# Pair 10 loaded before the last two x pieces, and the small matmuls of a spiking feed-forward kernel one place later

## What is computed

```
rates  = relu(x) * 0.001
c      = cond[:, None, :] + cumsum(rates, axis=1)
spikes = (floor(c) - floor(c one token earlier)) / 0.001
out    = x + relu(spikes @ w1 + b1) @ w2 + b2        # w1 512x2048, w2 2048x512
```

## Time and profile before

| | us |
|---|---|
| median of 3 runs | 106.62 |
| lowest and highest run | 106.08, 106.63 |
| the profiled execution | 106.2 |
| its span | 104.4 |
| TensorE busy | 96.1 (92%) |
| VectorE busy | 66.5 (64%) |
| GpSimd busy | 43.2 (41%) |
| ScalarE busy | 35.4 (34%) |

### The profile page before, as it was taken

The page is one execution under the profiler, slowest core; times in us unless marked ns, Lnnn a source line. Parts: engine busy times, 40 slices in busy tenths (PEclk is TensorE's granted clock), DMA queues, the critical chain, the costliest instruction groups (busy, mean ns, idle before and its releaser), DMA issues.

```text
span 104.4 us, 1157 instructions
## 1 busy us (share of the span) xinstructions
PE 96.1 (92%) x370; PEld 53.5 (51%) x370; DVE 66.5 (64%) x142; ACT 35.4 (34%) x64; POOL 43.2 (41%) x44
## 2 busy tenths in 40 slices
PE   5999999999999994979999999999999999999910
PEld 5844444445544440624244373568999994444300
DVE  2528999988799999288949978899980011200020
ACT  2767525325461505589620000001964440000000
POOL 6340000000088500037329244199977858850030
PEclk9999999999999999999999999999999999999997
DMA  2999999999999999999996987209999999884001
GB/s 73 323 335 402 419 417 409 414 402 414 413 405 401 397 399 404 406 388 387 372 371 255 420 355 298 104 0 420 420 405 402 337 196 226 108 96 61 6 6 61
DMA packets 10028, 31.66 MB, mean 303 GB/s; under 512 B 1671, under 2 KB 1799, under 8 KB 8994
## 3 DMA queue, kind: packets, MB, share of 16 engines
q1 hardware_dynamic: 8304, 29.63, 73.4%
q0 software_dynamic: 1568, 1.90, 11.0%
q10 hardware_dynamic: 146, 0.01, 0.1%
HBM read 21.58 MB, written 10.75 MB: 309 GB/s over the span
## 4 chain that ended last, share of the span: by engine, by line
DMA 25%; SPq 21%; DVE 14%; POOL 14%; issue 12%; PE 8%; ACT 2%; POOLq 0%; DVEq 0%
DMA w_sb<-in_w_pairs 16%; SPq L270 14%; DMA out<-x_sb 9%; POOL x_sb L352 8%; POOL out L345 5%; SPq L265 5%; DVE x_sb L672 4%; PE ps_table L805 4%; DVE same L599 3%; PE ps_idle L821 2%; DVE hot L618 1%; PE ps_idle L831 1%; POOL out L380 1%; PE ps_turn L842 1%; ACT w_sb L422 1%
## 5 line engine op out<-in xcount | busy, mean ns | idle before, releaser
L805 PE MATMUL ps_table<-w_sb 128*128 128x512 f32 x128 | 57.6, 597 | 1.5 <-ACT w_sb L422 1.5
L805 PEld LDWEIGHTS ps_table<-w_sb 128*128 128x128 f32 x128 | 23.4, 190 | 29.0 <-issue 23.9
L340 POOL DMA_INDIRECT rates<-in_x_turned,sixteen_at x8 | 9.9, 1235 | 34.2 <-DVE sixteen_at L562 32.4
L352 POOL TENSOR_TENSOR x_sb<-x_sb,idle_row 128x512 f32<-128x512 f32 x12 | 14.9, 1277 | 10.6 <-DVEq L704 3.7
L421 ACT ACTIVATE w_sb<-w_sb,b_col 128x512 f32<-128x512 f32 (+2 forms) x19 | 12.2, 642 | 17.6 <-DMA w_sb<-in_w_pairs 17.5
L548 DVE SCALAR_TENSOR_TENSOR total_two<-x_sb,total_two 128x1024 f32<-128x1024 f32 x14 | 17.2, 1225 | 0.9 <-DMA x_sb<-in_x 0.5
L893 PE MATMUL ps_table<-w_sb 128*128 128x512 f32 x32 | 14.0, 595 | 0.0
L345 POOL DMA_INDIRECT out<-w_sb,to_single x8 | 12.5, 1557 | 3.4 <-issue 1.8
L422 ACT ACTIVATE w_sb<-w_sb,minus_relu_b 128x512 f32<-128x512 f32 (+2 forms) x19 | 12.3, 649 | 0.6
L672 DVE TENSOR_TENSOR x_sb<-x_sb,ps_idle 128x2048 f32<-128x2048 f32 x5 | 11.2, 2282 | 1.5 <-ACT idle_row L447 1.3
L451 ACT ACTIVATE w_sb<-ps_turn,b_col 128x128 f32<-128x128 f32 x8 | 2.9, 368 | 20.9 <-PE ps_turn L886 20.9
(11 more groups left out here) (113 smaller groups left out, 66.1 us busy)
## 6 DMA issues: line engine op xcount, KB each, us to landing
x_sb<-in_x SPq DMA_DIRECT2D x16, 512.0 KB, 13.9
out<-x_sb SPq DMA_DIRECT2D x8, 1024.0 KB, 4.2
w_sb<-in_w_pairs SPq DMA_DIRECT2D x15, 512.0 KB, 15.5
w_sb<-in_w SPq DMA_DIRECT2D x4, 1024.0 KB, 15.3
w_sb<-in_w_pairs SPq DMA_DIRECT2D x2, 256.0 KB, 2.9
b_row<-in_b SPq DMA_DIRECT2D x1, 256.0 KB, 15.4
rates<-in_x_turned,sixteen_at POOLq DMA_INDIRECT x8
out<-w_sb,to_single POOLq DMA_INDIRECT x8
```

What stands on the lines that cost most here:

```text
L340: pool.indirect_dma_start(out=rates[:, col, :], out_offset=None, in_=x_sixteen, in_offset=bass.IndirectOffsetOnAxis(ap=sixteen_at[:, col:c ...
L352: last = pool.tensor_tensor(x_sb[b][:, t, :], x_sb[b][:, t, :], idle_row[:, :], ALU.add)
L805: last = pe.matmul(ps_table[c][:, :], table_hidden[:, m, c * P:(c + 1) * P], w2_sb[:, m, :], start=(m == 0), stop=(m == FC - 1))
```

## The change

It reorders; nothing is added or taken away.

- SyncE's loads: pair 10 comes after x piece 13, ahead of pieces 14 and 15. The pairs from 11 on come behind piece 15 as before. The stores of batch 0 go 0, 3, 1, 2 instead of 0, 2, 3, 1.
- TensorE: the sums of batch 1 come after three parts of chunk 10 instead of one. The first spread comes after the whole of chunk 11, instead of after chunk 10, and the strips right behind it. The join comes after one part of chunk 12, the first count of leads after three parts of chunk 12. From chunk 13 on, all is as before.
- VectorE: step 8 of the idle row by hand goes between x pieces 13 and 14, ahead of the last two pieces. The quarter of tokens 8 to 11 of batch 0 goes from ahead of the second tokens to behind the second spikes, so that one quarter is added ahead of the second tokens.
- GpSimd adds 2, 2 and 8 single tokens after its three gates, instead of 3, 2 and 7.

```diff
@@ SyncE, loads @@
-            for h in range(13, B * XH):
-                load_x(h)
-            for m in range(10, FC):
+            load_x(13)
+            load_pair(10)
+            load_x(14)
+            load_x(15)
+            for m in range(11, FC):
                 load_pair(m)
@@ SyncE, stores @@
-            for b, q in ((0, 0), (0, 2), (0, 3), (0, 1), (1, 3), (1, 0), (1, 1), (1, 2)):
+            for b, q in ((0, 0), (0, 3), (0, 1), (0, 2), (1, 3), (1, 0), (1, 1), (1, 2)):
@@ GpSimd @@
             pool.wait_ge(reading_psum, 1)
-            add_idle(0, 12, 15)
+            add_idle(0, 12, 14)
             pool.wait_ge(reading_psum, 2)
-            add_idle(0, 15, 16)
-            add_idle(1, 12, 13)
+            add_idle(0, 14, 16)
             pool.wait_ge(reading_psum, 3)
-            add_idle(1, 13, 16)
+            add_idle(1, 12, 16)
             add_idle(1, 8, 12)
@@ VectorE @@
             find_bases(0)
-            block_totals(1, 5, XH)
+            block_totals(1, 5, 6)
             idle_by_hand(8)
+            block_totals(1, 6, XH)
             find_blocks(1)
@@
             add_idle(0, 0, 4)
-            add_idle(0, 8, 12)
             find_tokens(1)
@@
             add_idle(0, 4, 8)
             second_spikes()
+            add_idle(0, 8, 12)
             add_idle(1, 0, 4)
@@ TensorE @@
             table_chunk(9)
-            table_part(10, 0, 1)
+            table_part(10, 0, 3)
             sum_totals(1)
-            table_part(10, 1, DC)
+            table_part(10, 3, DC)
+            table_chunk(11)
             spread_tokens(0)
-            table_part(11, 0, 2)
             add_strips(0, FC - BY_HAND + 1)
-            table_part(11, 2, 3)
+            table_part(12, 0, 1)
             join_strips()
-            table_part(11, 3, DC)
-            table_part(12, 0, 1)
+            table_part(12, 1, 3)
             count_leads(0)
-            table_part(12, 1, DC)
+            table_part(12, 3, DC)
             table_part(13, 0, 3)
             spread_tokens(1)
```

## The result

The changed kernel takes 104.55 us (median of 5 runs, 103.89 to 104.73), the kernel before 106.08 (5 runs, 105.89 to 106.63): a ratio of 0.984, interval 0.9805 to 0.9875. A second set of the same kernel, with before on the same chip, gave 104.31 against 106.30, ratio 0.9846 (0.9801 to 0.9892). By medians it is faster by 1.5 and 2.0 us, by the ratios by 1.6 to 1.7, where 2.9 were forecast. The forecast 103.5 is about 1 us too low, and the measured time lies in the range. Medians in this document are over all executions; ratios leave out executions over 1.5% above the fastest of their kernel, which matters for the small sets (e3).

The account below looks back on a forecast made before the run. TensorE was taken to bound the kernel, with three stalls (1.66, 0.86, 0.36 us) adding to 2.88; the steps gave 2.92 less, span 101.5, time 103.3 or 103.7 by the median, stated as 103.5, range 102.9 to 105.1.

Parts of the forecast that it names:

- Step 1: Loads: pair 10 lands near 37.3, so TensorE's 1.66 us of idleness before chunk 10 goes, with 1.4 in hand.
- Step 2: VectorE's totals: done by 42.3 with 0.5 us cover, second sums on TensorE at 42.84 against 42.80, no gain there.
- Step 3: First spread and strips on TensorE: no wait for tokens, 1.0 us in hand, strips at 48.58, 0.84 earlier.
- Step 4: Join: still bound by strips and ScalarE, 2.87 us after the strips, so at 51.45; idle row's copy ends 53.21.
- Step 5: VectorE's one quarter ahead of second tokens: these come 3.04 us earlier, no TensorE wait, about 0.1 in hand at the count.
- The gather: Gather for the second tokens: lands at 55.3, 5.7 us after issue, against a start of 55.56; cost taken as 0.
- Step 6: From the second count of leads: old order, 5.73 us to the first layer, which starts at 68.27, 2.92 us earlier.
- Step 7: GpSimd and stores: last tile near 74.3, batch 1's scatters end near 93.5, last scatter with 4 us in hand.
- C: Rival: x piece 15 lands late and delays the second sums; 104 to 105.2 us, chance 0.09.
- D: Rival: no change, the stores set the end or the gaps return elsewhere; 106.6 us, chance 0.06.
- E: Rival: slower, piece 15 so late that the whole chain from the totals slips; 106.6 to 108.1 us, chance 0.06.
- B: Rival: second tokens late, by GpSimd's two tiles (first mechanism) or a late gather; 103.7 to 104.8 us, chance 0.17.

Follow-up runs that it names:

- e3: Changed kernel with the quarter of tokens 8 to 11 of batch 0 back ahead of the second tokens; 105.44 us, ratio 0.9885.
- e2: Changed kernel with the order of loads and VectorE's step 8 put back as before; 105.04 us, ratio 0.9888.
- e7: Kernel before with four more small unused matmuls on TensorE right behind the first sums of blocks; 106.39 us, ratio 1.0014.
- e8: Changed kernel with four more small unused matmuls on TensorE right behind the first sums of blocks; 105.75 us, ratio 0.9927.
- e4: Changed kernel with ScalarE's two steps on chunk 15 behind its two copies of the idle row; 103.89 us, ratio 0.9761.
- e11: Changed kernel with GpSimd's tiles 0, 2, 10 after its gates instead of 2, 2, 8; 103.97 us, ratio 0.9803.
- e6: The same program as e4, run again beside the changed kernel on a second chip; 104.80 us, ratio 0.9858.
- e9: Changed kernel with the join two parts of table later, behind three parts of chunk 12; 105.46 us, ratio 0.9943.
- e12: Changed kernel with later join, no quarter ahead of the second tokens, GpSimd's first gate (three tiles) at its old place; 107.71 us, ratio 1.0177.
- e10: Changed kernel with later join, no quarter ahead of the second tokens, GpSimd's first gate behind batch 0's slot rows; 105.29 us, ratio 0.9931.

## Why the prediction was right in kind and too large in size

The forecast was 2.92. In the two profiles themselves the account closes: less 0.91 at the join (3.78 instead of 2.87) that is 2.01, and 2.00 were measured from the first table matmul to the first layer; with the front 0.26 earlier (first sums at 25.29, not 25.55) the first layer is 2.26 earlier, and the span 2.3 shorter. Step by step:

- **Step 1 held.** ScalarE starts chunk 10 at 37.03 (forecast 37.3), and TensorE's 38 matmuls have no gap. But the term of 1.66 us was mis-sized for the median: it is what remains between TensorE's arrival and pair 10, and the profile of before came with an early arrival (first sums 25.55; the mean of 14 profiles is 25.96). With the mean it is about 1.2, and in e2 it was 0.75. The prediction took a wait for a constant of the kernel; it is a buffer, and e7 and e8 show the same work hidden in one kernel (+0.1) and paid in the other (+0.9 by the ratios).
- **Step 2 held.** Piece 15 waits 0.24 for its landing, totals end at 41.95, second sums at 42.49; counted from the first sums, 17.20 after them against 17.25 before.
- **Step 3 held.** First spread without a wait, strips at 48.21 (forecast 48.58; 0.26 of it from the earlier front).
- **Step 4 failed, in both profiles of the changed kernel.** "It stays bound by the strips and ScalarE: 49.42 to 52.29 before, 2.87; so 51.45." It was 48.21 to 51.99, 3.78, with 0.80 idle on TensorE. ScalarE's copy comes 3.1 us after the strips' start in such an execution, where 2.2 stood in the one profile of before. Of the eight profiles with the changed kernel's order of strips, one part of table and join, four are of this kind; in the others (e2, e3, e4, e11) the join starts 2.8 after the strips without a wait. It is worth 1.0 us when it happens. Why the strips have two values is open: ScalarE is excluded by e4 and e6, the records of TensorE's matmuls don't show it, and no run changed the strips themselves.
- **Step 5 held, with as little in hand as was said.** The long step of the tokens was forecast at 0.3 and was 0.23, behind GpSimd's tiles that end at 56.47; the count of leads started at 63.19 with no idleness in its row, 0.1 after the six matmuls ahead of it had their turn (60.51 + 6 x 0.429 = 63.08), and the leads were there at 63.08. One quarter more costs 2.0 us in the profile (e3), the join later 1.0 by the times (e9). e12 shows the same mechanism with three tiles: 2.7 us. The gather was no cost: in e10, where VectorE waits for nothing else, it lets the tokens start at 55.52, 5.6 after its last issue at 49.90; the forecast from the other gather was 5.7.
- **Step 6** follows: 63.19 to 68.93 is 5.74, forecast 5.73.
- **Step 7 was off in what it leaves.** GpSimd was to have its last tile at 74.3; it was at 65.14 + 9.93 = 75.07, since the third gate opened 2.3 earlier than before and not 3.0. Its scatters start at 76.98, after 1.92 of idleness, and those of batch 1 at 87.52 instead of about 86.4. The 3.79 in hand, forecast 4, were enough here and not in e10.
- **Sum.** 2.92, less about 0.4 for the front and about 0.5 for the join (1.0 in four of eight), leaves 2.0. Measured were 1.5 and 2.0 by medians, 1.6 to 1.7 by the ratios, whose intervals are 0.4 us wide to either side. How often the slow strips come outside the profiled executions is not known.

Of the rivals, C (piece 15 late) did not happen, nor D or E in the changed kernel. B's first mechanism, GpSimd's tiles beside the tokens, was there and cost 0.1 at most. The measured time fell among the times given for B, but mainly by causes that were not among the rivals: that it lies in the range is in part luck.

## What to carry to other kernels

A wait read from one profile is a buffer as well as a loss: before counting it as gain, look at what varies ahead of it, since the kernel without the wait pays for that from then on. A move tried alone can look worthless because the wait only changes its name: the loads alone gave 1.0019, with 1.11 us of waiting for totals in place of 1.49 for the pair. Whether they pay on top of the rest then has to be measured too; here it was 0.5 us, not clear of noise. A small set with an interval can mislead where a kernel's executions have two values: one program gave 0.9761 and 0.9858. And when work is pushed off one engine's path, read what the next chain has in hand at its end: here the last scatter's idleness went from 7.46 to 3.79 to none, and with none the earlier TensorE was worth nothing.

## What the runs showed of the hardware

- The first table matmuls stand 0.86 us apart in some executions and 0.43 in others, which puts TensorE about 1.2 us later at 25 us (first sums at 26.46 in e6, 25.29 in the changed kernel's first profile); the view of the granted clock shows 1.00 in both.
- One group of sixteen small matmuls with equal rows lets the next engine, idle and waiting, go 1.99 (e4) or 3.10 us (e6) after its start, in two executions of one kernel.
- VectorE's scan, and its single-input tensor_scalar in SBUF, wait for GpSimd's tensor_tensor as its two-input operations do: 1.29 and 0.95 us (e12) instead of 0.29 and 0.19 (e10).
- An indirect gather of 128 rows of 64 bytes, issued while the loads run, lets its reader start 5.6 us after its issue (e10, 49.90 to 55.52) and 5.7 (e12, 49.49 to 55.16).
